# One unit's steps in a new order on four engines, and the drain merged from them, in a two-layer attention and expert kernel

## The reference, cut to what matters

```python
x = L0_attn_x                      # 8 x 256 tokens of 256
xn = _layernorm(x)
x = x + _L0_attn_ref(xn, ...) + _L0_ffn_ref(xn, ...)
xn = _layernorm(x)
x = x + _L1_attn_ref(xn, ...) + _L1_ffn_ref(xn, ...)
# _L0_attn_ref, 16 heads of 128, delta rule, one token after another:
q = l2norm(causal_conv_silu(x @ Wq.T, conv_q)) * hd ** -0.5    # k too, v without the norm
pred  = einsum('bhd,bhdv->bhv', kt, state)
delta = bt[..., None] * (vt - pred)
state = state + einsum('bhd,bhv->bhdv', kt, delta)
ot    = einsum('bhd,bhdv->bhv', qt, state)
o = o * rsqrt(mean(o * o) + eps) * rms_w;  o @ Wo.T
# _L1_attn_ref: chunks of 64 tokens; three 128x128 weight matrices per head are
# updated per chunk by Newton-Schulz iterations, then applied to the queries
```

## Time and profile before

| | |
|---|---|
| median of 3 executions | 1775.88 us (1772.57 to 1785.23) |
| the profiled execution | 1781.47 us, of which the span from first to last instruction is 1779.7 us |
| mean granted TensorE clock | 0.979 of full speed |
| PE busy / PE weight loads | 1692.1 us (95% of the span) / 1247.5 us (70%) |
| DVE / ACT / POOL busy | 1470.7 (83%) / 1206.8 (68%) / 1104.7 us (62%) |

### The profile page before, as it was taken

The page is one execution under the profiler, slowest core; times in us unless marked ns, Lnnn a source line. Parts: engine busy times, 40 slices in busy tenths (PEclk is TensorE's granted clock), DMA queues, the critical chain, the costliest instruction groups (busy, mean ns, idle before and its releaser), DMA issues.

```text
span 1779.7 us, 41654 instructions
## 1 busy us (share of the span) xinstructions
PE 1692.1 (95%) x14070; PEld 1247.5 (70%) x14070; DVE 1470.7 (83%) x3684; ACT 1206.8 (68%) x2911; POOL 1104.7 (62%) x1148
## 2 busy tenths in 40 slices
PE   7999899999999999999999999999988788888888
PEld 5577567777777777777777777777767566666667
DVE  5322599999999999999999999999986788888863
ACT  2134477777777777777777777877754588778763
POOL 1600067777777777776666666666666478778841
PEclk9999999999999999999999999999986699999999
DMA  9433310111110110100001000101002000000033
GB/s 313 148 96 110 105 31 22 38 31 27 36 33 27 30 36 21 39 18 27 27 18 27 24 18 24 30 12 30 15 2 60 1 1 1 2 1 1 1 89 91
DMA packets 66098, 73.85 MB, mean 41 GB/s; under 512 B 10975, under 2 KB 54767, under 8 KB 65775
## 3 DMA queue, kind: packets, MB, share of 16 engines
q1 hardware_dynamic: 62919, 63.92, 12.2%
q0 software_dynamic: 3072, 8.65, 1.5%
HBM read 55.45 MB, written 17.10 MB: 41 GB/s over the span
## 4 chain that ended last, share of the span: by engine, by line
PE 84%; DVE 8%; ACT 5%; issue 1%; POOL 1%; SPq 0%; DMA 0%; POOLq 0%; DVEq 0%; ACTq 0%
PE banks L735 19%; PE banks L893 6%; PE banks L762 4%; PE banks L849 3%; PE banks L770 3%; PE banks L868 3%; PE banks L778 3%; PE banks L700 3%; PE banks L807 3%; PE banks L815 2%; PE banks L821 2%; PE banks L949 2%; PE banks L814 2%; PE banks L1025 2%; PE banks L719 2%; PE banks L960 2%
## 5 line engine op out<-in xcount | busy, mean ns | idle before, releaser
L735 PE MATMUL banks<-xnT,hw 128*128 128x512 f32 x768 | 414.1, 622 | 2.5 <-DVE cv L2034 2.5
L2090 DVE CAST_PREDICATED MM<-lmask,banks 128x512 bf16<-128x512 uint32 x384 | 272.5, 710 | 35.8 <-PE banks L815 31.5
L2034 DVE SCALAR_TENSOR_TENSOR cv<-banks,hc,cv 128x510 f32<-128x510 f32 (+2 forms) x384 | 284.8, 742 | 5.5 <-ACT cv L1439 0.8
L1503 ACT ACTIVATE T<-banks 128x256 bf16<-128x256 f32 x384 | 149.3, 389 | 147.4 <-PE banks L807 147.1
L2694 POOL TENSOR_TENSOR X<-X,yrow 128x512 f32<-128x512 f32 x128 | 163.3, 1276 | 66.3 <-ACT yrow L1535 66.3
L2658 POOL TENSOR_TENSOR kn<-nsum,half_pos 128x4 f32<-128x4 f32 x64 | 65.6, 1025 | 142.2 <-DVE nsum L2059 142.2
L815 PEld LDWEIGHTS banks<-MM,T 128*128 128x128 bf16 x1536 | 104.3, 98 | 65.4 <-issue 48.4
L814 PEld LDWEIGHTS banks<-T,MM 128*128 128x128 bf16 x1280 | 99.1, 97 | 65.3 <-ACT T L1503 63.1
L2034 DVE SCALAR_TENSOR_TENSOR cv<-banks,hcv,cv 128x510 f32<-128x510 f32 (+2 forms) x192 | 141.4, 736 | 1.4 <-ACT cv L1439 1.3
L893 PE MATMUL banks<-ho,OT 128*128 128x256 f32 x512 | 141.7, 400 | 0.0
L807 PEld LDWEIGHTS banks<-MM,Gb 128*128 128x128 bf16 x1536 | 84.2, 98 | 81.3 <-issue 43.7
(11 more groups left out here) (318 smaller groups left out, 4885.9 us busy)
## 6 DMA issues: line engine op xcount, KB each, us to landing
MM<-in_eye SPq DMA_DIRECT2D x64, 256.0 KB, 2.7
slot_rows<-zeros SPq DMA_DIRECT2D x1, 5304.0 KB, 20.1
xs<-slot_rows SPq DMA_DIRECT2D x13, 408.0 KB, 4.0
slot_out<-ye SPq DMA_DIRECT2D x13, 384.0 KB, 2.7
hw<-in_hw SPq DMA_DIRECT2D x16, 256.0 KB, 3.4
wT<-in_winit SPq DMA_DIRECT2D x8, 384.0 KB, 3.9
wgu<-in_wgu SPq DMA_DIRECT2D x1, 2816.0 KB
w1c<-in_ew SPq DMA_DIRECT2D x16, 176.0 KB
```

The lines of the kernel that those rows point to most:

```text
L735: ins = pe.matmul(PROJ[t][:], hw[:, kk, t, :], xnT[:, kk, u.b * BLK:(u.b + 1) * BLK], start=(kk == 0), stop=(kk == KD - 1))
L1503: act.activation(strips(T1[:].rearrange("p i t -> p (i t)"), LEVELS[lv], 0, 1), grams_bank(u)[:, 0:TILES * 64].rearrange("p (k e) -> p k e ...
L2034: dve.scalar_tensor_tensor(o, y, taps_of(t)[:, TAPS - 1 - i:TAPS - i], o, ALU.mult, ALU.add).then_inc(dve_conv, 1)
L2090: dve.copy_predicated(dst, m, ps).then_inc(dve_mm, 1)
```

## The change

Each engine's `period` is turned to begin at another step, and `units` takes the number of ages that it gives. Turning alone changes no order. What changes in a unit's order is this.

- PE: `correct(u3, 1, 0)` before `project(KEY, 0)`; `invert(u1, 4)` before `correct(u2, 0, 1)`.
- ACT: `gram_half` before the query's `tap0`; `first_queries` before `finish_inverse`; `second_queries` after `square_output`; the query's silu after `mean_squares`; both `scaled_rows` before `invert(.., 3)`.
- DVE: `gram(u1, 0)` before `refine(u3, 1, 0)`.
- POOL: `add_rows(.., 0)` and `first_rhs` later; `mask` before `root`, and `mask` and `gram_rest` for a unit that is a period older; `gram_rest` between the two `add_rows`; fetching and adding the experts' rows at other places.
- SP: one more wait, for the last unit's inversion, before the start weights of the fourth pair are loaded. PE: two waits for work that is done in time (`act_ot`, `ln_kept0` and `ln_kept1`).
- The drain lists hold the same steps, with these neighbours exchanged and some others: `second_turn` and `turn_qk(x0)` earlier, `gates(x0)` and `hidden_back(x0)` a step earlier, `carry` later (PE); `norm_qk(x0, 1)` and `(x0, 2)` before `residual(a63, 0, 1)` (DVE); on POOL both `add_rows(a61, ..)` behind `rhs_minus(a62, 1, 1)`, and `add_squares(a63)` before `rate_powers(1)`. POOL's list now begins at a59.

```diff
@@ sync
             sp.wait_ge(*weights_loaded(2))
+            sp.wait_ge(pe_inv, 13 * UNITS)
             load_weights(3)
@@ tensor, period
                 do(invert, u2, 8)
+                do(correct, u3, 1, 0)
                 do(project, unbegun(u0), KEY, 0)
-                do(correct, u3, 1, 0)
                 do(invert, u2, 9)
@@
                 do(project_out, u3, 0)
+                do(invert, u1, 4)
                 do(correct, u2, 0, 1)
-                do(invert, u1, 4)
                 do(project_out, u3, 1)
@@ scalar, period (as it stands after)
+                do(keep_values, u2)
+                do(invert, u2, 2)
+                do(mean_squares, u4)
+                do(silu, unbegun(u1), QRY)
+                do(silu, unbegun(u1), KEY)
+                do(scaled_rows, u4, 0)
+                do(scaled_rows, u4, 1)
+                do(invert, u2, 3)
+                do(keep_first, u3, 1)
                 do(silu, u1, VAL)
+                do(invert, u2, 4)
                 do(square_queries, u1)
                 do(invert, u2, 5)
                 do(cross_keys, u1)
+                do(gram_half, u1)
                 do(tap0, unbegun(u0), QRY)
-                do(gram_half, u1)
                 do(invert, u2, 6)
@@ vector, period
                 do(key_scales, u1)
+                do(gram, u1, 0)
                 do(refine, u3, 1, 0)
-                do(gram, u1, 0)
                 do(gram, u1, 1)
@@ gpsimd, period
-                do(add_squares, u3)
-                do(rhs_minus, u2, 0, 1)
-                do(inverse_rms, u3)
-                do(add_rows, u3, 0)
-                do(rhs_minus, u2, 1, 0)
-                do(first_rhs, u1)
-                do(root, u0)
-                do(mask, u1)
-                do(rhs_minus, u2, 1, 1)
-                do(add_rows, u3, 1)
-                do(gram_rest, u0)
-                if 0 <= i <= TOP0 * NT:
-                    do(rows_added, u3)
-                merge(i)
-                do(rhs_minus, u1, 0, 0)
+                u0, u1, u2, u3, u4, u5, u6 = units(h, j, 7)
+                do(add_squares, u5)
+                do(rhs_minus, u4, 0, 1)
+                do(inverse_rms, u5)
+                fetch_rows(i - 3)
+                do(rhs_minus, u4, 1, 0)
+                do(mask, u4)
+                add_fetched_rows(i - 4, u6, 1)
+                do(root, u2)
+                do(first_rhs, u3)
+                do(rhs_minus, u4, 1, 1)
+                fetched_rows_added(i - 4)
+                do(add_rows, u5, 0)
+                do(gram_rest, u3)
+                do(add_rows, u5, 1)
+                do(rhs_minus, u3, 0, 0)
@@ gpsimd, drain
             inverse_rms(a61)
+            rhs_minus(a62, 1, 0)
+            mask(a62)
+            first_rhs(a63)
+            rhs_minus(a62, 1, 1)
             add_rows(a61, 0)
-            rhs_minus(a62, 1, 0)
-            first_rhs(a63)
-            mask(a63)
-            rhs_minus(a62, 1, 1)
+            gram_rest(a63)
             add_rows(a61, 1)
             rate_powers(0)
@@
             add_rows(a62, 1)
+            add_squares(a63)
             rate_powers(1)
-            add_squares(a63)
             norm_root(2, 1)
```

More of the change, by code:

```diff
@@ L279, in unit, with units @@
             return Unit(n, d % NBLK, h + d // NBLK)
-        def units(h, j):
-            return [unit(h, j, back) for back in range(5)]
+        def units(h, j, backs):
+            return [unit(h, j, back) for back in range(backs)]
         def do(step, u, *which):
@@ L411, in build @@
         x12, x13, x14, x15 = (Pair(n, n // NP, n % NP) for n in range(STEPS - NP, STEPS))
-        a60, a61, a62, a63 = (Unit(n, n % NBLK, n // NBLK) for n in range(UNITS - NBLK, UNITS))
+        a59, a60, a61, a62, a63 = (Unit(n, n % NBLK, n // NBLK) for n in range(UNITS - 5, UNITS))
         a_const = sem("attn_constants")
@@ L958, in project_qk @@
                     pe.wait_ge(t_wk2, u.n - NP + 1)
+                else:
+                    pe.wait_ge(ln_kept0, NBLK + u.p + 3)
+                    pe.wait_ge(ln_kept1, NBLK + u.p + 3)
                 for kk in range(KD):
@@ L1183, in _ @@
             pe.wait_ge(*t_half)
-            invert(a62, 5)
-            gram_keys(a63)
-            invert(a62, 6)
-            first_solve(a61, 1)
-            gram_second(a63)
             times_gram(a61, 1, 0)
@@ L1211, in _ @@
             project_out(a61, 0)
+            invert(a63, 4)
             correct(a62, 0, 1)
-            invert(a63, 4)
             project_out(a61, 1)
+            second_turn(0, 0)
             carry(a62)
             invert(a63, 5)
-            second_turn(0, 0)
+            second_turn(0, 1)
             invert(a63, 6)
             first_solve(a62, 1)
-            second_turn(0, 1)
             times_gram(a62, 1, 0)
@@ L1242, in _ @@
             project_out(a62, 1)
-            carry(a63)
             second_turn(1, 0)
             second_turn(1, 1)
+            carry(a63)
+            turn_qk(x0)
             first_solve(a63, 1)
-            turn_qk(x0)
             times_gram(a63, 1, 0)
@@ L1251, in _ @@
             turn_v(x0)
+            gates(x0)
             times_gram(a63, 1, 1)
-            gates(x0)
+            hidden_back(x0)
             correct(a63, 1, 1)
-            hidden_back(x0)
             outputs(a63)
@@ L1721, in _ @@
             act.wait_ge(t_const, 5 * 16)
+            keep_values(a62)
+            invert(a62, 2)
+            mean_squares(a60)
+            silu(a63, QRY)
+            silu(a63, KEY)
+            scaled_rows(a60, 0)
+            scaled_rows(a60, 1)
+            invert(a62, 3)
+            keep_first(a61, 1)
             silu(a63, VAL)
+            invert(a62, 4)
             square_queries(a63)
@@ L1738, in _ @@
             scaled_rows(a61, 0)
+            scaled_rows(a61, 1)
             invert(a63, 3)
-            scaled_rows(a61, 1)
             keep_first(a62, 1)
@@ L2117, in period @@
             def period(h, j):
-                u0, u1, u2, u3, u4 = units(h, j)
+                u0, u1, u2, u3, u4 = units(h, j, 5)
+                do(invert, u2, 1)
+                do(square_sums, u4)
+                do(residual, u3, 0, 1)
+                do(tap, u1, VAL, 1)
+                do(refine, u3, 0, 1)
+                do(invert, u2, 2)
+                do(tap, u1, VAL, 2)
                 do(second_rhs_half, u3)
@@ L2144, in period @@
                 do(refine, u2, 0, 0)
-                do(invert, u1, 1)
-                do(square_sums, u3)
-                do(residual, u2, 0, 1)
-                do(tap, u0, VAL, 1)
-                do(refine, u2, 0, 1)
-                do(invert, u1, 2)
-                do(tap, u0, VAL, 2)
             dve.wait_ge(a_const, 3 * 16)
@@ L2409, in gate_logits @@
                 dve.tensor_tensor(lg[:], lg[:], lmx[:].unsqueeze(2).to_broadcast([1, NB, E1]), ALU.subtract).then_inc(dve_once, 1)
+            invert(a62, 1)
+            square_sums(a60)
+            residual(a61, 0, 1)
+            tap(a63, VAL, 1)
+            refine(a61, 0, 1)
+            invert(a62, 2)
+            tap(a63, VAL, 2)
             second_rhs_half(a61)
@@ L2421, in _ @@
             key_scales(a63)
+            gram(a63, 0)
             refine(a61, 1, 0)
-            gram(a63, 0)
             gram(a63, 1)
@@ L2458, in _ @@
             square_sums(a62)
-            residual(a63, 0, 1)
             norm_qk(x0, 1)
             norm_qk(x0, 2)
+            residual(a63, 0, 1)
             refine(a63, 0, 1)
@@ L2822, in _ @@
             pool.memset(euler, float(np.e))
+            add_squares(a59)
+            rhs_minus(a60, 0, 1)
+            inverse_rms(a59)
+            rhs_minus(a60, 1, 0)
+            mask(a60)
+            root(a62)
+            first_rhs(a61)
+            rhs_minus(a60, 1, 1)
+            add_rows(a59, 0)
+            gram_rest(a61)
+            add_rows(a59, 1)
+            rhs_minus(a61, 0, 0)
+            add_squares(a60)
+            rhs_minus(a61, 0, 1)
+            inverse_rms(a60)
+            rhs_minus(a61, 1, 0)
+            mask(a61)
+            root(a63)
+            first_rhs(a62)
+            rhs_minus(a61, 1, 1)
+            add_rows(a60, 0)
+            gram_rest(a62)
+            add_rows(a60, 1)
+            rhs_minus(a62, 0, 0)
             add_squares(a61)
```

57 lines of the change are left out of this document (26 added, 31 removed).

## The result

The changed kernel takes **1826.5 us** in the median of 4 executions (1813.34 to 1832.1), the kernel before 1775.42: ratio 1.0274, 95% interval 1.0210 to 1.0338. It is slower, as forecast, but by 51 us instead of 22, and outside the range. The profiled execution took 1830.89 us (span 1829.1), 49.4 more than that of before.

What follows compares the result with a forecast made beforehand. PE's own work was taken to bound the steady state, DVE and POOL the drain. 14.4 (60 units at 0.24) + 2.3 + 5.5 = 22.2 us on 1775.9 gave 1798.1 us, 1.25% slower; range 1775 to 1814.

Steps and rivals of the forecast that it cites:

- PE bound, hardly a wait to gain, an order can only cost: Steady state: PE's own work sets 17.41 us per unit, its waits total 0.2 us; an order costs more easily than gains.
- POOL in the period: cost 0: POOL's reordered steps in the period: idle 30%, results made a step ahead or right after their input, so cost 0.
- PE's swaps and DVE's `gram`, cost 0 with a bound of 0.2: Period, before correct and times_gram: the matmul in between covers moved waits, cost 0; without cover, 0.2 us.
- ACT's tap, 0.20: Period: gram_half first makes the query's tap 0.46 us late; after slack, PE waits 0.20 us for MM per unit.
- my slack of 0.26: DVE's idle time before refine in the query's tap chain, 0.26 us, taken to absorb part of the 0.46 delay.
- Scaled rows, 0.04: Period, ACT: both scaled_rows ahead of level 3's T make PE's L814 wait for T, 0.04 us per unit.
- `rate_powers(1)`, 5.5: Drain, POOL: the power behind add_squares(a63) starts 5.5 us later, delaying rates_end on DVE; all shows, 5.5 us.
- Rows of a61, 2.3: Drain, POOL: later additions of a61's rows delay DVE's norm_stats and the chain to Rb; 2.3 us, bounds 0 and 2.4.
- 2, the waits add up: Rival for the period: slack of 0.26 is gone, each unit grows 0.46 us or more, total 1811; chance 0.10.
- 3: Rival for the drain: earlier steps fill PE's waits and halve the time at 1.2 GHz, 23 us less, 1753; chance 0.09.
- the distance of 17.65: Sign in the steady state: two L860 (PE's carry) in the middle are 17.65 us apart instead of 17.41.
- the wait at L807: Sign in the period: PE waits on L807 for DVE's MM, which the tap's delay makes 0.20 us late.

Runs made afterwards that it cites:

- kernel 1: Changed kernel with POOL's mask behind root instead of ahead of it, in the period only: 1814.86 us, ratio 1.0200 to the kernel before.
- kernels 4 and 5: Kernel before with one edit each: 4, POOL's mask ahead of first_rhs and root, 1781.8 us; 5, PE's correct ahead of project(KEY, 0), 1779.2 us.
- kernel 7: Changed kernel with POOL's mask behind root and DVE's gram(u1, 0) behind refine(u3, 1, 0) again: 1808.69 us, ratio 1.0174 to the kernel before.
- kernel 3: Changed kernel with ACT's first tap of the query ahead of gram_half again: 1828.98 us, ratio 1.0275 to the kernel before.
- kernel 12: Changed kernel with three drain exchanges undone, tap, refine and mask orders put back, and POOL's addition of fetched rows behind both add_rows: 1787.39 us, ratio 1.0056.
- kernel 15: The changed kernel measured once more, without any edit: 1823.34 us, ratio 1.0280 to the kernel before.
- kernel 8: As kernel 7, and besides ACT's first tap of the query ahead of gram_half again: 1810.31 us, ratio 1.0189 to the kernel before.

## Why the prediction was right and wrong

- **PE bound, hardly a wait to gain, an order can only cost:** right, and so was the sign. DVE's 95% was the warning that counted: it is the engine through which each of the three parts came.
- **"POOL in the period: cost 0":** this is the step that failed. I argued from POOL's 30% of idle time and from who needs its results, and so looked for waits alone. But `mask` costs by where it stands, beside an instruction of DVE that doesn't need it: 0.30 us in each late unit, 17.92 to 17.62 (kernel 1). I had the sign of it before me: in the earlier trace rows the `rates_end` of 1.14 us ends at 1352.58, with POOL's addition in the earlier trace rows (1352.54), where its twin takes 0.18. I read it as contention in the drain and never asked it of the period.
- **PE's swaps and DVE's `gram`, cost 0 with a bound of 0.2:** the cover was named (the `project` in between), but the price without it was taken from the longest wait of a kernel that has the cover. Measured: 0.38 idle in front of `correct`, by the swap and the mask together (kernels 4 and 5 lose 0.09 and 0 with one of them), and 0.14 for `gram`.
- **ACT's tap, 0.20:** the mechanism was right, the size was not. With the two other causes gone (kernel 7, late units) DVE waits 0.35 us for `cv`, not 0.45; less my slack of 0.26 that leaves 0.09, and 0.08 was measured, at the very place I named. Beside the others it costs 0 (kernel 3).
- **Scaled rows, 0.04:** 0 in sum (kernel 12). I had the wrong waiter: what stands right behind the rows is `gram_keys`, not `T`.
- **`rate_powers(1)`, 5.5:** right in kind. DVE waited 5.18, 4.0 came through.
- **Rows of a61, 2.3:** DVE waits 1.22 us for `X` there; its part was not measured alone. **Not priced at all:** `rate_keys` ahead of `Rm`, 3.7 us. It stands in the full diff; my list of the change has it only under "some others", and I passed it over.
- **Rivals:** 2, the waits add up, came nearest (0.46 in each unit, 1811). PE's `correct` waits, as it had it, but for a held `key_norms` and not through the lost slack. 3 is refuted: PE's waits grew. The two stretches above, at 0.74 and 0.66, begin 5 us later than the carry of unit 61, those of the earlier trace rows with it; cut from that carry on the clock is 0.76 and 0.66, where it was 0.85 and 0.61. Over the 123 us together it is 0.71 in the changed kernel and 0.74 in its repeat (kernel 15), with 0.74 before. The Trainium skill's rule beside that rival (TensorE: Matmul & The Clock Gate, HAM oscillation), that gaps bring the clock down, is neither borne out nor refuted by that.
- **The signs I named:** the distance of 17.65 did not come (17.92), nor the wait at L807. DVE's idle time before the tap came at 0.20 for 0.45. The idle time before `refine` did go, and for the reason I gave: with the tap back in its old place it is there again, in kernel 3 although `key_norms` is still held, and in kernel 8. The clock of the first stretch moved by 0.09, near my bound of 0.1. The waits for `lgt` (5.18), for `X` (1.22 for 2) and PE's longer one before `ln_row` came.

In sum: 60 x (0.50 - 0.24) = 16 us too little in the units and 14.0 - 7.8 = 6 in the drain. That makes 44 us of the 51 between the medians (47.5 for kernel 15). The other 3 to 7 us are not traced; single executions of one kernel lie 13 to 19 us apart.
